# Kept experts: one output array for all scatters, each waiting for the last, in place of two arrays and a join

## The chip, the core and the metric

The kernel runs on one core of a Trainium2 chip. The metric is device time in microseconds (us); lower is better. TensorE (PE) multiplies, VectorE (DVE) and ScalarE (ACT) work element by element, GpSimd (POOL) does so too and builds the descriptors of indirect DMAs, SyncE (SP) issues plain DMAs.

## The reference, cut to what matters

The program is a network of four layers over 4096 tokens of 256 values: attention, a mixture of experts, a linear attention, and a second mixture of experts with 48 kept experts. Only the last one is touched in its arithmetic's order. With `T = 4096`, `CAP = 96`, `TOP_K = 8`:

```python
xb = zeros((E, CAP + 1, H)).at[flat_e, pos_c].set(x[tok])   # up to 96 tokens for each expert
g, u = split(einsum('ech,eoh->eco', xb, gate_up_proj), 2)
out = einsum('eci,ehi->ech', silu(g) * u, down_proj)
final = zeros_like(x).at[tok].add(y * w[:, None])           # a token may belong to 8 experts
x = x + final
```

So each expert's 96 rows are added to rows of one sum, and rows of different experts can be the same token.

## The kernel before

`front_phase` is the first part of the first mixture of experts. Its SP program loads weights, then clears rows of DRAM from the zeroed tile `front_zero`: the 96 spare rows of `out` and of `rows` (L889, L890), and the whole array `odd` (trace name `odd_sums`; L892 and L894, 4192 rows of 256 values). After them SP stores eight pieces of `roots` (L898), each once ACT has made it. At the phase's end SP waits for the clearing to have landed.

`ranking_phase` writes each token's row (256 values and its 48 weights) to `rows` (trace name `token_rows`), writes `x` to `out`, and makes `idx`, the list of 96 token numbers of each expert; places that are not used point to spare rows.

`kept_experts_phase` is the program's last phase. For each expert e of 48:

- POOL gathers 96 rows of `rows` into `xg` (L2860), six experts ahead of the scatter that stands before it in POOL's program;
- SP loads the expert's two weights, `kept_GU` of 192 KB and `kept_DN` of 96 KB, into one of 8 slots (L2844, L2845), once PE has used the slot's last ones (`pe_y`);
- PE transposes the rows (L2900), multiplies them by `GU` (L2910), then by `DN` (L2919); ACT copies and takes the silu; DVE makes `h` and then the weighted result `ys` (L2972);
- POOL scatters the 96 rows of `ys` with an add into DRAM (L2868): even experts into `out`, odd experts into `odd`.

POOL's program is written out in full: six gathers, then for each e: wait, scatter e, gather e+6 (none for the last six). The adds of one array must not overlap, since the same row may be in both; so scatter e waits for scatter e-2, the last one to the same array:

```python
if e >= 2:
    pool.wait_ge(added[e % 2], 16 * (e // 2))
scatter(e)
```

After the last scatter POOL waits for both arrays and issues four DMAs that add `odd` to `out` (L2887, 1 MB each), the join, and waits for them. The phase then ends with the semaphores' clearing and a barrier.

Of the kernel before, what the change touches and what calls it, by code (L numbers as in the profile page):

```python
# [16 lines left out]
F32 = mybir.dt.float32  # L17
# [4 lines left out]
ALU = mybir.AluOpType  # L22
# [4 lines left out]
D = 256  # L27
KD = D // P
BATCH, SEQ = 4, 1024
T = BATCH * SEQ  # L30
# [10 lines left out]
def done(step):  # L41

    return step + 1 + CREDIT
# [40 lines left out]
LH, LBLK = 16, 128  # L84
# [709 lines left out]
NW = LAT + SHARED  # L794


def front_phase(nc, a, AO, X, LH, LL, first_w, roots, ident, out, odd, rows):

    E, G, N = EXPERTS, GROUPS_E, PER_GROUP
    TAKEN = -3.0e38  # L800
# [3 lines left out]
    with Phase(nc, "front") as ph:  # L804
# [11 lines left out]
        zero = ph.sb("zero", [SPARE, ROW])  # L816
# [60 lines left out]
        @block.sync  # L877
        def _(sp):
            sp.dma_start(wo[:], a["L0_attn_W_O"].rearrange("(k p) n -> p k n", p=P)).then_inc(wo_in, 16)
            sp.dma_start(wu[:, :, 0:LAT], a["L0_ffn_fc1_w"].rearrange("(k p) n -> p k n", p=P)).then_inc(wu_in, 16)  # L880
            sp.dma_start(wu[:, :, LAT:NW], a["L0_ffn_shared_up_w"].rearrange("(k p) n -> p k n", p=P)).then_inc(wu_in, 16)
            sp.dma_start(wg[:], a["L0_ffn_gate_w"].rearrange("(k p) n -> p k n", p=P)).then_inc(wg_in, 16)
            sp.dma_start(down[:], a["L0_ffn_shared_down_w"].rearrange("(s p) n -> p s n", p=P)).then_inc(down_in, 16)
            sp.dma_start(bias_b[:, 0, :], a["L0_ffn_gate_bias"].rearrange("(o e) -> o e", o=1).to_broadcast([P, E]))\
                .then_inc(bias_in, 16)
            for to, source in first_w:
                sp.dma_start(to, source).then_inc(first_in, 16)
            sp.wait_ge(zeroed, 1)
            sp.dma_start(out[T:T + SPARE, :], zero[:, 0:D]).then_inc(cleared, 16)  # L889
            sp.dma_start(rows[T:T + SPARE, :], zero[:]).then_inc(cleared, 16)  # L890
            blank = zero[:, 0:D].rearrange("p (o n) -> p o n", o=1)
            sp.dma_start(odd[0:BLANKS * SPARE, :].rearrange("(t p) n -> p t n", p=SPARE),  # L892
                         blank.to_broadcast([SPARE, BLANKS, D])).then_inc(cleared, 16)
            sp.dma_start(odd[BLANKS * SPARE:T + SPARE, :], zero[0:T + SPARE - BLANKS * SPARE, 0:D])\  # L894
                .then_inc(cleared, 16)
            for c in range(CHUNKS):
                sp.wait_ge(act_ro, c + 1)
                sp.dma_start(roots[c], rootT[:, c % 2]).then_inc(stored[c % 2], 16)  # L898
            sp.wait_ge(first_in, 16 * len(first_w))
            sp.wait_ge(cleared, 64)  # L900
            sp.wait_ge(stored0, 8 * CHUNKS)
            sp.wait_ge(stored1, 8 * CHUNKS)

# [673 lines left out]
                out(2 * CHUNKS + half, half)  # L1577


def latent_moe_layer(nc, a, X, AO, held, ident, out, odd, rows):  # L1580

    with ExitStack() as c:
        LH = c.enter_context(nc.sbuf_tensor("B_LH", [P, T], F32R))
        LL = c.enter_context(nc.sbuf_tensor("B_LL", [P, T], F32R))
        wraw = c.enter_context(nc.sbuf_tensor("B_wraw", [P, 2, 2, WG, P], F32))
        fc2 = c.enter_context(nc.sbuf_tensor("B_fc2", [P, D], F32))
        roots = nc.dram_tensor("B_roots", (CHUNKS, EXPERTS, CHUNK), F32, kind="Internal").ap()
        views = (a["L0_ffn_w1"].rearrange("e l i -> l e i"), a["L0_ffn_w2"].rearrange("e i l -> i e l"))
        first = [(wraw[:, 0, w], views[w][:, 0:WG, :]) for w in range(2)]
        first += [(fc2[:], a["L0_ffn_fc2_w"])]  # L1590
        front_phase(nc, a, AO, X, LH, LL, first, roots, ident, out, odd, rows)
        held.close()
        W1H, W1L, W2H, W2L = (c.enter_context(nc.sbuf_tensor(f"B_{n}", [P, EXPERTS, P], F32R))
                              for n in ("W1H", "W1L", "W2H", "W2L"))
        experts_phase(nc, X, LH, LL, roots, views, wraw, fc2, W1H, W1L, W2H, W2L)
# [732 lines left out]
        linear_attention_phase(nc, X, XH, XL, ident, raw, wo_raw, dec_in, w_qkv, w_gate, w_out,  # L2328
                               a["L1_attn_rms_weight"], decays, kdec, bdec, acc, rs, x_rows, x_first, sums, later)
KEPT, OLD, WIDTH, CAP, TOP_D = 48, 128, 96, 96, 8  # L2330
BLANKS = (T + 96) // 96
ROW = D + KEPT
SLOTS = 8
JOINS = 4


def ranking_phase(nc, raw, o2n, x_first, acc, rs, sums, ident, rows, out, idx):
# [476 lines left out]
            tt(idx[:], tok[:], unused[:], ALU.add)  # L2814


def kept_experts_phase(nc, a, rows, out, odd, idx, ident):

    gu = a["L1_ffn_gate_up_proj"]
    dn = a["L1_ffn_down_proj"]  # L2820
# [1 line left out]
    with Phase(nc, "kept") as ph:  # L2822
# [9 lines left out]
        YP = ph.ps("YP", [CAP, 2, 512])  # L2832
        w_in = [ph.sem(f"w_in{u}") for u in range(S)]
        g_in = [ph.sem(f"g_in{u}") for u in range(S)]
        (pe_x, act_x, pe_gu, act_g, dve_h, pe_y, dve_y, added0, added1, joined, pool_turns) = ph.sems(
            "pe_x act_x pe_gu act_g dve_h pe_y dve_y added0 added1 joined pool_turns")
        added = (added0, added1)
        sums = (out, odd)
        block = ph.block()

        @block.sync
# [13 lines left out]
        @block.gpsimd  # L2855
        def _(pool):
            def gather(e):
                u = e % S

                nc.gpsimd.indirect_dma_start(out=xg[:, u], out_offset=None, in_=rows,  # L2860
                                             in_offset=bass.IndirectOffsetOnAxis(ap=idx[:, e:e + 1], axis=0))\
                    .then_inc(g_in[u], 16)

            def scatter(e):

                pool.wait_ge(dve_y, done(e))  # L2866

                nc.gpsimd.indirect_dma_start(out=sums[e % 2],  # L2868
                                             out_offset=bass.IndirectOffsetOnAxis(ap=idx[:, e:e + 1], axis=0),
                                             in_=ys[:, e % S], in_offset=None, compute_op=ALU.add)\  # L2870
                    .then_inc(added[e % 2], 16)

            for e in range(S - 2):
                gather(e)
            for e in range(KEPT):
                if e >= 2:
                    pool.wait_ge(added[e % 2], 16 * (e // 2))
                scatter(e)
                if e + S - 2 < KEPT:
                    gather(e + S - 2)  # L2880
            for u in range(S):
                pool.wait_ge(g_in[u], 16 * (KEPT // S))  # L2882
            for s in added:
                pool.wait_ge(s, 16 * (KEPT // 2))  # L2884
            parts = T // JOINS
            for j in range(JOINS):
                nc.gpsimd.dma_start(out[j * parts:(j + 1) * parts, :], odd[j * parts:(j + 1) * parts, :],  # L2887
                                    accum_op=ALU.add, max_dma_last_dim=8192).then_inc(joined, 16)
            pool.wait_ge(joined, 16 * JOINS)

        @block.tensor
        def _(pe):
# [80 lines left out]
                        .then_inc(dve_y, 1)  # L2973


def capacity_moe_layer(nc, a, x_first, ident, out, odd, rows, acc, rs, sums, raw, o2n):
    with ExitStack() as c:
        idx = c.enter_context(nc.sbuf_tensor("D_idx", [CAP, KEPT], U32))
        ranking_phase(nc, raw, o2n, x_first, acc, rs, sums, ident, rows, out, idx)
        kept_experts_phase(nc, a, rows, out, odd, idx, ident)  # L2980
def build_program(nc, a, out):
    x = a["L0_attn_x"].rearrange("b s d -> (b s) d")
    with ExitStack() as ctx:
        def keep(name, shape, dt=F32):
            return ctx.enter_context(nc.sbuf_tensor(name, shape, dt))

        X = keep("X", [P, TILES, D])
        x_at = nc.sbuf_base - TILES * D * 4
        ident = keep("ident", [P, P])
        kdec = keep("kdec", [P, LH])  # L2990
        bdec = keep("bdec", [P, LH])
        decays = nc.dram_tensor("decays", (LH, P, 2, LBLK), F32).ap()
        rows = nc.dram_tensor("token_rows", (T + SPARE, ROW), F32, kind="Internal").ap()
        odd = nc.dram_tensor("odd_sums", (T + SPARE, D), F32, kind="Internal").ap()
        held = ExitStack()
        AO = attention_layer(nc, a, x, X, held, ident, decays, kdec, bdec)
        latent_moe_layer(nc, a, X, AO, held, ident, out, odd, rows)
        raw = keep("D_w_gate", [P, KD, OLD])
        o2n = keep("D_o2n", [P, 1], I32)
        acc = nc.alloc_sbuf_tensor_at("C_acc", [P, TILES, D], F32, offset=x_at)  # L3000
        rs = keep("C_rs", [P, TILES])
        x_first = keep("D_x_first", [P, 2 * BATCH, D])
        sums = (keep("D_stats", [P, TILES, 6]), keep("D_mv", [P, TILES, 2]), keep("D_std", [P, TILES]),
                keep("D_rstd", [P, TILES]), keep("D_shift", [P, TILES]))
        x_rows = nc.dram_tensor("x_rows", (T, D), F32, kind="Internal").ap()
        linear_attention_layer(nc, a, X, ident, decays, kdec, bdec, acc, rs, raw, o2n, x_rows, x_first[:], sums)
        capacity_moe_layer(nc, a, x_first, ident, out, odd, rows, acc, rs, sums, raw, o2n)

# [3 lines left out]
SPARE = 96  # L3014
# [22 lines left out]
```

## Time and profile before

| | |
|---|---|
| median of 3 runs | 2849.91 us (2849.21 to 2852.32) |
| the profiled execution's own time | 2849.45 us |
| its span | 2847.1 us |
| PE busy | 2624.2 us (92%) |
| DVE busy | 1706.1 us (60%) |
| ACT busy | 1410.0 us (50%) |
| POOL busy | 786.6 us (28%) |
| last phase, from its first gather at 2666.94 us to the span's end | 180.2 us |

The busy shares are of the whole span; the change touches the last phase and some DMAs of the front phase, at about 606 us. There the stretches' own rows count, not the shares above.

### The profile page before, as it was taken

To read this page: it belongs to the slowest core of one execution; us is meant where nothing else is said; L and a number is where in the kernel's file an instruction comes from. 1 tells how busy PE (TensorE), PEld (TensorE's weight loads), DVE (VectorE), ACT (ScalarE), POOL (GpSimd) and SP (SyncE) were. 2 spreads that over 40 slices of the span, in tenths; PEclk is the share of its full clock that TensorE was granted. 3 is DMA by queue.
4 is the path that set the end of the run, shared out by engine and by line. 5 is a ranking of instruction groups with operands and counts; after the bars stand their busy time and mean duration, and the time that the engine had idled before them with its cause. 6 is when DMAs were issued, how large, how long until landed. Compare 5 with 4: busy or idle time off the path is not lost. (4 is left out here: it accounts for less than half of the span.)

```text
span 2847.1 us, 49896 instructions
## 1 busy us (share of the span) xinstructions
PE 2624.2 (92%) x17120; PEld 2103.3 (74%) x17120; DVE 1706.1 (60%) x3301; ACT 1410.0 (50%) x2606; POOL 786.6 (28%) x802
## 2 busy tenths in 40 slices
PE   7899999979979999899999999999999999986573
PEld 6444444448758888689998998989899899974452
DVE  7688888726678888665545545454544545567321
ACT  6477777766648878644333333333333333336310
POOL 3521212210052222122222222222222222224574
PEclk9799999989989999899999999999999999997665
DMA  8964645030055545422222222222222222223476
GB/s 253 214 109 63 84 70 81 14 102 3 4 194 179 192 184 189 139 49 50 74 50 59 53 60 49 49 61 51 58 50 66 46 50 61 47 74 124 115 169 125
DMA packets 409864, 260.98 MB, mean 92 GB/s; under 512 B 255904, under 2 KB 372032, under 8 KB 400896
## 3 DMA queue, kind: packets, MB, share of 16 engines
q1 hardware_dynamic: 401392, 243.59, 33.9%
q0 software_dynamic: 8256, 14.52, 3.0%
q8 instruction: 134, 2.20, 0.3%
q14 instruction: 82, 0.67, 0.1%
HBM read 182.09 MB, written 80.14 MB: 92 GB/s over the span
## 5 line engine op out<-in xcount | busy, mean ns | idle before, releaser
L1799 POOL TENSOR_TENSOR lin_o2sum<-lin_o2sum,lin_o 128x512 f32<-128x512 f32 x128 | 184.4, 1440 | 959.3 <-ACT lin_o L1863 959.3
L738 DVE TENSOR_REDUCE score_pm<-score_SM 128x1 f32<-128x512 f32 (+3 forms) x608 | 364.3, 655 | 80.6 <-PE score_SM L598 47.6
L692 ACT ACTIVATE score_PR<-score_SE 128x512 f32<-128x512 f32 (+1 forms) x640 | 309.7, 558 | 106.1 <-PE score_SE L626 102.4
L2136 DVE TENSOR_TENSOR C_acc<-lin_OUT,C_acc 128x512 f32<-128x512 f32 x240 | 165.2, 691 | 231.4 <-PE lin_OUT L1997 229.6
L1953 PE MATMUL lin_PJ<-C_XH,lin_WH 128*128 128x512 f32 x768 | 252.9, 410 | 2.1 <-DVE C_XL L2164 2.1
L1840 ACT ACTIVATE lin_qT<-lin_PJ 128x512 f32<-128x512 f32 x128 | 76.5, 598 | 353.5 <-PE lin_PJ L1953 353.5
L1953 PE MATMUL lin_PJ<-C_XL,lin_WH 128*128 128x512 f32 x768 | 240.7, 395 | 0.0
L598 PE MATMUL score_SM<-A_KR,A_QR 96*128 96x512 bf16 (+3 forms) x768 | 229.7, 340 | 11.7 <-DVEq L81 9.2
L1953 PE MATMUL lin_PJ<-C_XH,lin_WL 128*128 128x512 f32 x768 | 237.4, 390 | 0.0
L1868 ACT ACTIVATE lin_goh<-lin_go 128x512 fp32r<-128x512 f32 x128 | 81.0, 633 | 267.9 <-DVE lin_go L2272 267.9
L626 PE MATMUL score_SE<-A_QR,A_KR 99*128 99x512 bf16 (+3 forms) x768 | 210.4, 330 | 2.0 <-ACT score_PR L692 1.5
L2174 DVE STREAM_TRANSPOSE lin_kblk<-lin_kT 128x512 f32<-128x512 f32 x112 | 79.7, 711 | 214.8 <-ACT lin_kT L1844 214.5
L2063 PE MATMUL lin_O<-lin_sd,lin_v 128*128 128x128 f32 x1024 | 190.8, 276 | 9.8 <-POOL lin_qd L1794 4.2
L1499 ACT ACTIVATE experts_h<-experts_z 128x512 f32<-128x512 f32 x256 | 161.1, 629 | 70.7 <-DVE experts_z L1404 67.2
L1794 POOL TENSOR_TENSOR lin_qd<-lin_qT,lin_dec 128x512 f32<-128x512 f32 x128 | 165.0, 1289 | 72.0 <-DVE lin_dec L2236 72.0
L1404 DVE SCALAR_TENSOR_TENSOR experts_z<-experts_HP,experts_sq 128x512 f32<-128x512 f32 x256 | 173.9, 685 | 17.4 <-PE experts_HP L1536 14.3
L2063 PEld LDWEIGHTS lin_O<-lin_sd,lin_v 128*128 128x128 f32 x1024 | 158.2, 191 | 20.8 <-issue 13.7
L2066 PE MATMUL lin_O<-lin_qd,lin_kv 128*128 128x128 f32 x896 | 173.2, 275 | 0.0
L565 POOL TENSOR_SCALAR_AFFINE_SELECT score_PR<-score_PR 128x512 f32<-128x512 f32 x128 | 79.7, 635 | 333.5 <-ACT score_PR L692 333.5
L1953 PEld LDWEIGHTS lin_PJ<-C_XH,lin_WL 128*128 128x128 f32 x768 | 144.5, 188 | 34.1
L1953 PEld LDWEIGHTS lin_PJ<-C_XL,lin_WH 128*128 128x128 f32 x768 | 144.5, 188 | 34.0
L1411 DVE TENSOR_TENSOR experts_hl<-experts_h,experts_hh 128x512 fp32r<-128x512 f32 x192 | 139.1, 724 | 33.6 <-ACT experts_hh L1500 24.3
(372 smaller groups left out, 6488.7 us busy)
## 6 DMA issues: line engine op xcount, KB each, us to landing
experts_sq<-B_roots SPq DMA_DIRECT2D x64, 1024.0 KB, 4.7
k_turned<-lin_kblk SPq DMA_DIRECT2D x112, 256.0 KB, 2.0
lin_krow<-k_turned SPq DMA_DIRECT2D x448, 64.0 KB, 2.4
A_QR<-q_parts SPq DMA_DIRECT2D x96, 128.0 KB
A_KR<-k_parts SPq DMA_DIRECT2D x96, 128.0 KB
kept_GU<-L_ffn_gate_up_proj SPq DMA_DIRECT2D x48, 192.0 KB
v_rows<-inp_vt SPq DMA_DIRECT2D x32, 256.0 KB, 4.2
A_V<-v_rows SPq DMA_DIRECT2D x16, 512.0 KB
```

The costliest lines, as they stand in the source:

```text
L598: ins = nc.tensor.matmul(SM[:, count % RING, at:at + nk], QR[0:ROWS_QK, u, h0 + j, t * P:(t + 1) * P], KR[0:ROWS_QK, u, h0 + j, k0:k0 + nk ...
L626: ins = nc.tensor.matmul(SE[:, e % RING, at:at + nq], KR[0:ROWS_ALL, u, h, kt * P:(kt + 1) * P], QR[0:ROWS_ALL, u, h, q:q + nq], start=Tru ...
L692: nc.scalar.activation(PR[:, st % BUFS, h, 0:width], SE[:, e % RING, 0:width], ACT.Exp, scale=SCALE)\
L738: nc.vector.tensor_reduce(pm[:, n % 2, h0:h0 + nh, t, k0 // CHUNK], SM[:, count % RING, 0:nh * nk].rearrange("p (h k) -> p h k", h=nh), AX ...
L1404: nc.vector.scalar_tensor_tensor(z[:, e % 2], HP[:, e % BUFS], 0.0, sq[:, (e // QE) % BUFS, e % QE], ALU.max, ALU.mult).then_inc(dve_z, 1)
L1499: nc.scalar.activation(h[:, e % BUFS], z[:, e % 2], ACT.Square).then_inc(act_h, 1)
L1794: nc.gpsimd.tensor_tensor(qd[:], qT[:, j], dec[:, j, 0:1, :].to_broadcast([P, B4, BLK]), ALU.mult).then_inc(pool_qd, 1)
L1799: nc.gpsimd.tensor_tensor(o2sum[:, c], o2sum[:, c], o2[:], ALU.add).then_inc(pool_sum, 1)
L1953: ins = nc.tensor.matmul(PJ[:, bank], a[:, w, k, j * DH:(j + 1) * DH], x[:, k, :, c, :], start=(n == 0), stop=(n == 3 * KD - 1))
L2063: ins = nc.tensor.matmul(O[:, b, :], v[:, c % 2, b, j * DH:(j + 1) * DH], sd[:, b, :], start=True, stop=(c == 0))
L2066: ins = nc.tensor.matmul(O[:, b, :], kv[:, j, b, :], qd[:, b, :], start=False, stop=True)
L2136: nc.vector.tensor_tensor(dst, OUT[:, half], dst, ALU.add).then_inc(dve_acc[half], 1)
```

## The change

Every expert's scatter goes into `out`, and scatter e waits for scatter e-1. The array `odd` is gone, and with it the two DMAs that cleared it and the four that added it to `out`.

```diff
@@ front_phase, SP
             sp.dma_start(out[T:T + SPARE, :], zero[:, 0:D]).then_inc(cleared, 16)
             sp.dma_start(rows[T:T + SPARE, :], zero[:]).then_inc(cleared, 16)
-            blank = zero[:, 0:D].rearrange("p (o n) -> p o n", o=1)
-            sp.dma_start(odd[0:BLANKS * SPARE, :].rearrange("(t p) n -> p t n", p=SPARE),
-                         blank.to_broadcast([SPARE, BLANKS, D])).then_inc(cleared, 16)
-            sp.dma_start(odd[BLANKS * SPARE:T + SPARE, :], zero[0:T + SPARE - BLANKS * SPARE, 0:D])\
-                .then_inc(cleared, 16)
...
-            sp.wait_ge(cleared, 64)
+            sp.wait_ge(cleared, 32)
@@ kept_experts_phase, POOL
                 pool.wait_ge(dve_y, done(e))
 
-                nc.gpsimd.indirect_dma_start(out=sums[e % 2],
+                nc.gpsimd.indirect_dma_start(out=out,
                                              out_offset=bass.IndirectOffsetOnAxis(ap=idx[:, e:e + 1], axis=0),
                                              in_=ys[:, e % S], in_offset=None, compute_op=ALU.add)\
-                    .then_inc(added[e % 2], 16)
+                    .then_inc(added, 16)
...
             for e in range(KEPT):
-                if e >= 2:
-                    pool.wait_ge(added[e % 2], 16 * (e // 2))
+                if e:
+                    pool.wait_ge(added, 16 * e)
                 scatter(e)
                 if e + S - 2 < KEPT:
                     gather(e + S - 2)
             for u in range(S):
                 pool.wait_ge(g_in[u], 16 * (KEPT // S))
-            for s in added:
-                pool.wait_ge(s, 16 * (KEPT // 2))
-            parts = T // JOINS
-            for j in range(JOINS):
-                nc.gpsimd.dma_start(out[j * parts:(j + 1) * parts, :], odd[j * parts:(j + 1) * parts, :],
-                                    accum_op=ALU.add, max_dma_last_dim=8192).then_inc(joined, 16)
-            pool.wait_ge(joined, 16 * JOINS)
+            pool.wait_ge(added, 16 * KEPT)
```

This is how POOL's program ends before the change: the last two gathers, the last seven scatters with two destinations in turn, then the join.

```order
L2860 DMA kept_xg<-token_rows,D_idx 96x304
L2868 DMA odd_sums<-kept_ys,D_idx 4192x256
L2860 DMA kept_xg<-token_rows,D_idx 96x304
L2868 DMA out<-kept_ys,D_idx 4192x256
L2868 DMA odd_sums<-kept_ys,D_idx 4192x256
L2868 DMA out<-kept_ys,D_idx 4192x256
L2868 DMA odd_sums<-kept_ys,D_idx 4192x256
L2868 DMA out<-kept_ys,D_idx 4192x256
L2868 DMA odd_sums<-kept_ys,D_idx 4192x256
L2887 DMA out<-odd_sums 128x2048 x4
```

And this is the same place after it, in which the scatter's line is L2859 and the gather's L2851.

```order
L2851 DMA kept_xg<-token_rows,D_idx 96x304
L2859 DMA out<-kept_ys,D_idx 4192x256
L2851 DMA kept_xg<-token_rows,D_idx 96x304
L2859 DMA out<-kept_ys,D_idx 4192x256 x6
```

The order of gathers and scatters is the same; every scatter has one destination, so two in a row always share it, and nothing stands behind the last one.

## Rows read from the trace of the kernel before

**Rows 1.** Busy us (count) of PE, PEld, DVE, ACT, POOL; PEclk, DMA share, GB/s, one stretch:

```profile
2700.00:2740.00 40.00, 28.77 (x163) 20.95 (x163) 8.47 (x27) 6.28 (x27) 32.06 (x27) 0.71 0.80 175
```

**Rows 2.** POOL in order of time: start, duration, line, names, idle before and its releaser:

```profile
2678.99 1.52 POOL L2868 DMA_INDIRECT out<-kept_ys,D_idx  x1 [4.71 <-DVE kept_ys L2972]
...
2702.93 1.44 POOL L2868 DMA_INDIRECT out<-kept_ys,D_idx  x1 [0.30 <-issue]
...
2714.85 1.44 POOL L2868 DMA_INDIRECT out<-kept_ys,D_idx  x1 [0.30 <-issue]
...
2720.81 1.44 POOL L2868 DMA_INDIRECT out<-kept_ys,D_idx  x1 [0.31 <-DVE kept_ys L2972]
2722.55 0.93 POOL L2860 DMA_INDIRECT kept_xg<-token_rows,D_idx  x1 [0.30 <-issue]
2723.79 1.44 POOL L2868 DMA_INDIRECT odd_sums<-kept_ys,D_idx  x1 [0.31 <-DVE kept_ys L2972]
...
2804.25 1.44 POOL L2868 DMA_INDIRECT out<-kept_ys,D_idx  x1 [0.30 <-issue]
2805.99 1.43 POOL L2868 DMA_INDIRECT odd_sums<-kept_ys,D_idx  x1 [0.31 <-issue]
2807.90 1.40 POOL L2868 DMA_INDIRECT out<-kept_ys,D_idx  x1 [0.48 <-DMA out<-kept_ys,D_idx]
2809.81 1.40 POOL L2868 DMA_INDIRECT odd_sums<-kept_ys,D_idx  x1 [0.51 <-DMA odd_sums<-kept_ys,D_idx]
2812.06 1.40 POOL L2868 DMA_INDIRECT out<-kept_ys,D_idx  x1 [0.85 <-DVE kept_ys L2972]
2814.05 1.40 POOL L2868 DMA_INDIRECT odd_sums<-kept_ys,D_idx  x1 [0.58 <-issue]
```

**Rows 3.** The scatter's line, all 48: one of its waits (us, times), and issue to landing:

```profile
  DMA out<-kept_ys,D_idx: 0.5, 1
...
DMA to landing us min/median/max: 3.3/3.5/4.8
```

**Rows 4.** The chain that ended last, at the last scatter: start us, us, what:

```profile
2814.05 3.42 DMA odd_sums<-kept_ys,D_idx
...
2817.53 0.55 issue
```

**Rows 5.** The join's line: duration ns, first and last start; issue to landing:

```profile
L2887 POOL DMA_DIRECT2D out<-odd_sums x4: 919/1272/1492, 2818.1 to 2820.3; - x4
...
DMA to landing us min/median/max: 8.2/14.7/20.7
```

**Rows 6.** The page's first line:

```profile
span 2847.1 us, 49896 instructions
```

**Rows 7.** Landings of the scatters issued from 2702.9 to 2711.9 us (four):

```profile
DMA to landing us min/median/max: 4.1/4.3/4.6
```

**Rows 8.** The same for 2714.9 to 2729.7 us (six):

```profile
DMA to landing us min/median/max: 3.5/3.6/3.9
```

**Rows 9.** The same for 2804.2 to 2814.1 us (the last six):

```profile
DMA to landing us min/median/max: 3.3/3.4/3.4
```

**Rows 10.** SP's queue, the kept experts' weight loads in order of time:

```profile
2703.91 0.38 SPq L2844 DMA_DIRECT2D kept_GU<-L_ffn_gate_up_proj  x1
...
2717.30 0.38 SPq L2844 DMA_DIRECT2D kept_GU<-L_ffn_gate_up_proj  x1
```

**Rows 11.** SP's queue in the front phase:

```profile
606.47 13.91 SPq L894 DMA_DIRECT2D odd_sums<-front_zero  x1
697.86 102.40 SPq L898 DMA_DIRECT2D B_roots<-front_rootT  x8
```

**Rows 12.** Waits of 595 to 720 us: us in total, times, longest us:

```profile
PE front_TR L935 <- DVE front_AL L1166: 6.4, 1, 6.4
ACT front_WOH L1115 <- DMA front_wo<-L_attn_W_O: 5.2, 1, 5.2
```

More of the change, by code:

```diff
@@ L794, with front_phase @@
 NW = LAT + SHARED
-def front_phase(nc, a, AO, X, LH, LL, first_w, roots, ident, out, odd, rows):
+def front_phase(nc, a, AO, X, LH, LL, first_w, roots, ident, out, rows):
     E, G, N = EXPERTS, GROUPS_E, PER_GROUP
@@ L1577, in _, with latent_moe_layer @@
                 out(2 * CHUNKS + half, half)
-def latent_moe_layer(nc, a, X, AO, held, ident, out, odd, rows):
+def latent_moe_layer(nc, a, X, AO, held, ident, out, rows):
     with ExitStack() as c:
@@ L1590, in latent_moe_layer @@
         first += [(fc2[:], a["L0_ffn_fc2_w"])]
-        front_phase(nc, a, AO, X, LH, LL, first, roots, ident, out, odd, rows)
+        front_phase(nc, a, AO, X, LH, LL, first, roots, ident, out, rows)
         held.close()
@@ L2330 @@
 KEPT, OLD, WIDTH, CAP, TOP_D = 48, 128, 96, 96, 8
-BLANKS = (T + 96) // 96
 ROW = D + KEPT
 SLOTS = 8
-JOINS = 4
 def ranking_phase(nc, raw, o2n, x_first, acc, rs, sums, ident, rows, out, idx):
@@ L2814, in _, with kept_experts_phase @@
             tt(idx[:], tok[:], unused[:], ALU.add)
-def kept_experts_phase(nc, a, rows, out, odd, idx, ident):
+def kept_experts_phase(nc, a, rows, out, idx, ident):
     gu = a["L1_ffn_gate_up_proj"]
@@ L2834, in kept_experts_phase @@
         g_in = [ph.sem(f"g_in{u}") for u in range(S)]
[L2835 to L2838, printed above, removed]
+        (pe_x, act_x, pe_gu, act_g, dve_h, pe_y, dve_y, added) = ph.sems(
+            "pe_x act_x pe_gu act_g dve_h pe_y dve_y added")
         block = ph.block()
@@ L2973, in _, with capacity_moe_layer @@
                         .then_inc(dve_y, 1)
-def capacity_moe_layer(nc, a, x_first, ident, out, odd, rows, acc, rs, sums, raw, o2n):
+def capacity_moe_layer(nc, a, x_first, ident, out, rows, acc, rs, sums, raw, o2n):
     with ExitStack() as c:
@@ L2979, in capacity_moe_layer @@
         ranking_phase(nc, raw, o2n, x_first, acc, rs, sums, ident, rows, out, idx)
-        kept_experts_phase(nc, a, rows, out, odd, idx, ident)
+        kept_experts_phase(nc, a, rows, out, idx, ident)
 def build_program(nc, a, out):
@@ L2993, in build_program @@
         rows = nc.dram_tensor("token_rows", (T + SPARE, ROW), F32, kind="Internal").ap()
-        odd = nc.dram_tensor("odd_sums", (T + SPARE, D), F32, kind="Internal").ap()
         held = ExitStack()
         AO = attention_layer(nc, a, x, X, held, ident, decays, kdec, bdec)
-        latent_moe_layer(nc, a, X, AO, held, ident, out, odd, rows)
+        latent_moe_layer(nc, a, X, AO, held, ident, out, rows)
         raw = keep("D_w_gate", [P, KD, OLD])
@@ L3006, in build_program @@
         linear_attention_layer(nc, a, X, ident, decays, kdec, bdec, acc, rs, raw, o2n, x_rows, x_first[:], sums)
-        capacity_moe_layer(nc, a, x_first, ident, out, odd, rows, acc, rs, sums, raw, o2n)
+        capacity_moe_layer(nc, a, x_first, ident, out, rows, acc, rs, sums, raw, o2n)
 TRANSPOSED = ("L0_attn_W_Q", "L0_attn_W_K", "L0_attn_W_V", "L0_attn_W_O", "L0_ffn_gate_w", "L0_ffn_fc1_w",
```

## The prediction

> **What bounds the kernel now.** The change touches two places, so I read two stretches and not the shares of the whole span. First the chain of work that ended last: its end lies in the last phase, so what this phase gains or loses comes straight off the time. Then the busy table of a steady stretch of that phase [rows 1]. POOL is busy for 32.06 of 40 us, PE for 28.77, and neither alone looks full. POOL in order of time explains it [rows 2]: scatter 1.44 us, a gap of 0.30, gather 0.93, a gap of 0.31, next scatter. From 2720.81 to 2723.79 that is 2.98 us for an expert, and the gaps are put down to issuing or to a result that had come in the meantime. POOL issues back to back; it is the bound of this phase, and PE follows it. The first scatter starts at 2678.99, the last, 47 intervals later, at 2814.05: 135.06 us. Of these the last five, with no gather between, take 9.80 us (from 2804.25).
>
> The waits at the scatter's line come third: POOL waited there for an earlier scatter into the same array only at the very end, once in each array, the one shown being 0.5 us [rows 3]. With two arrays the wait is hidden: two intervals of 2.98 are 5.96 us, while a scatter lands 3.3 to 4.8 us after its issue, 3.5 in the median [rows 3]. That this is counted from the start of POOL's instruction and not from its end is seen in the chain: the last scatter starts at 2814.05 and its DMA takes 3.42 us, to 2817.47 [rows 4].
>
> **The change part by part.**
>
> *The new wait.* Scatter e may now start only when scatter e-1 has landed and POOL has noticed. Between the two stands one gather, whose 2.98 us no longer cover it. The new interval is landing L plus waking w. The trace has two such intervals in pure form, in the tail, where a scatter waited for the one of its own array: 2804.25 to 2807.90 is 3.65 us, and 2805.99 to 2809.81 is 3.82 [rows 2]. The landings there are 3.3 to 3.4 [rows 9], so w is about 0.25 and 0.42. Other wakings after a real pause: 0.55 us of issue behind the last landing [rows 4], and the scatter at 2812.06 with 0.85 us idle [rows 2]. I take w = 0.35, bounds 0.25 and 0.75.
>
> L is longer in the loop than in the tail. Read one by one, 13 of the 48 landings are 4.0 us or more; the other 35 average 3.5, all together 3.7. A group of each sort: 4.1 to 4.6 [rows 7] and 3.5 to 3.9 [rows 8]. What differs is when SP issues the next weights. In the first group that is about 1 us after the scatter (2702.93 and 2703.91), in the second about 2.4 us after (2714.85 and 2717.30) [rows 2, 10]; a load that falls into the scatter's own transfer stretches it by some 0.7 us. When SP issues depends on PE, which follows the gather issued right behind an earlier scatter; with another interval this offset changes, in a direction that I cannot fix. So I keep the mix of before, L = 3.7, and the interval is 3.7 + 0.35 = 4.05 us. Bounds: 3.65 from below, the shortest serial interval of the trace, and 3.7 + 0.75 = 4.45 from above.
>
> A rule speaks against this sum. The Trainium skill, page "DMA: Bandwidth & Descriptors", section "Anatomy of one DMA — SWDGE (gpsimd) path", gives a DMA issued from GpSimd about 2.0 us plus its bytes over 436 GB/s; 96 rows of 1 KB would by it take 2.2 us. If that ran from the issue, the gather would cover the wait and the loop would cost nothing. The trace has no landing below 3.3 us from the start of the instruction. Less POOL's 1.44 us there remain about 2 us, so the rule agrees with the trace only as the part behind POOL's own work. The row decides.
>
> The five last intervals have neither gathers nor loads beside them: the mean of the two pure ones, 3.74 us, each. Sum of the loop: 42 x 4.05 + 5 x 3.74 = 170.1 + 18.7 = 188.8 us, against 135.06: **+53.7 us**.
>
> What is queued behind the waiting scatter on POOL: gather e+6. It is issued right behind scatter e, so it comes later by the same delay; but it is six experts ahead, more than 24 us at the new pace, and what an expert needs from gather to `ys` is a landing of about 3.5 us and a few us of PE. Nobody waits that did not wait anyway. PE has 28.77 us of work in 40 now, and gets a third more time for each expert; even if its clock were granted lower more of the time than the 0.71 of now [rows 1], it stays behind POOL. Weight loads wait for PE, not the other way round. The eight slots of `ys` are not filled: DVE's result is then ready long before its scatter.
>
> *The join.* Its wait, its four DMAs and their landing go. The last of the four is issued at 2820.3, the longest landing is 20.7 us, that is 2841.0 [rows 5]; the span ends at 2847.1 [rows 6], so 6.1 us of closing stand behind it. From the last scatter's start to the span's end are now 33.05 us. After the change it is the landing of 3.4 and the same 6.1: 9.5 us. **-23.5 us**.
>
> *The clearing.* Two DMAs of SP in the front phase, of 4.1 MB together, go. The longer issue is 13.91 us on SP, but SP's next work is at 697.86 [rows 11], 77 us after it ended; this hides it. Who waited for a DMA there: ACT for `front_wo`, 5.2 us [rows 12], a load that stands ahead of the clearing in SP's queue and had landed before it began. PE's longest wait, 6.4 us, is for DVE, which followed ACT. I cost it at 0; without that cover it would be at most those 6.4 us, as a gain.
>
> *Sum.* 53.7 - 23.5 - 0 = +30.2 us on the profiled execution of 2849.45. The median of the runs is 2849.91, 0.46 above it, so the forecast is 2849.91 + 30.2 = **2880.1 us**, 1.1% slower. A measurement of this kernel tells 0.2% (5.7 us) from no change.
>
> **The rivals.**
>
> *The landings grow shorter (27 in 100).* A third more time for an expert thins the traffic (DMA share 0.80 now [rows 1]), and if the loads miss the scatter, L is 3.5 and the interval 3.85: 42 x 3.85 + 18.7 = 180.4, +45.3 - 23.5 = +21.8, 2871.7 us. At the lower bound, 47 x 3.65 = 171.6, it is +13.0, 2862.9.
>
> *The loads fall on every scatter (10 in 100).* PE's steps set when SP issues; if the offset locks at 1 us, L is 4.3 as in [rows 7] and the interval 4.65: 195.3 + 18.7 = 214.0, +78.9 - 23.5 = +55.4, 2905.3 us. Against it: in the trace of before the offset moved with PE's clock and no lock lasted. The same cost comes from waking always at its upper bound: 42 x 4.45 + 5 x 4.15 = 207.7, +49.1, 2899.0.
>
> *The wait is covered and the join's removal remains (3 in 100).* A landing below 2.98 - 0.25 = 2.7 us would leave the loop as it is: -23.5 us, 2826.4. This is the time by the rule above if it is counted from the issue. The mechanism decides from an interval of 2.87 + 23.5/47 = 3.37 us, 2.87 being the mean of the 47 now: below it the change is faster. The shortest serial interval of the trace is 3.65, in the tail where nothing else ran, and it would need a landing 0.3 us shorter than any of the 48.
>
> *The clearing did cost something (2 in 100).* Then up to 6.4 us come back at about 614 us: 2873.7. Against it stands the order of the waits above.
>
> **How the numbers follow.** My forecast has 58 in 100, with 27, 10, 3 and 2 for the others. The range runs from the shortest serial interval, 2863, to the upper bound of the waking, 2898; it takes in the first and the last rival, and leaves out half of the second, the third, and a little of the forecast's own margin at the ends. Faster by over 0.2%: 0.03. Within it, intervals of about 3.25 to 3.5 us: 0.01. Slower: 0.96.
>
> **What the changed kernel's profile would show.** POOL idle before nearly every scatter by about 1.4 us, released by the DMA of the scatter before (interval 4.05 less 2.98, and the usual 0.3); the last scatter near 2868 us; POOL's busy share down in the phase and PE's with it; no line for the join, and about 9.5 us from the last scatter to the end; the front phase the same, with SP's two issues gone. I am wrong in the size if the landings' median is far from 3.5 to 3.7, or the gap from landing to start far from 0.35; I am wrong in kind if POOL does not wait at the scatters, if the end behind the last one is much over 10 us, or if everything behind 620 us begins earlier.

## The result and the profile after

The changed kernel takes 2872.72 us (median of 4 runs, 2869.3 to 2873.57), the kernel before 2849.56 on the same chip: a ratio of 1.0075 [1.0063, 1.0088]. It is 23 us slower; 30 were forecast, in a range of 13 to 48.

The profiled execution took 2873.57 us, its span is 2871.9, 24.8 more than in [rows 6]. Where it went is read at three points of GpSimd's program: POOL in order of time, the changed kernel, with the same columns as [rows 2].

```profile
2680.72 1.52 POOL L2859 DMA_INDIRECT out<-kept_ys,D_idx  x1 [4.59 <-DVE kept_ys L2957]
...
2747.53 1.44 POOL L2859 DMA_INDIRECT out<-kept_ys,D_idx  x1 [1.19 <-DMA out<-kept_ys,D_idx]
2749.27 0.93 POOL L2851 DMA_INDIRECT kept_xg<-token_rows,D_idx  x1 [0.30 <-issue]
2751.24 1.44 POOL L2859 DMA_INDIRECT out<-kept_ys,D_idx  x1 [1.03 <-DMA out<-kept_ys,D_idx]
...
2841.44 1.44 POOL L2859 DMA_INDIRECT out<-kept_ys,D_idx  x1 [0.89 <-DMA out<-kept_ys,D_idx]
2844.99 1.43 POOL L2859 DMA_INDIRECT out<-kept_ys,D_idx  x1 [2.11 <-DMA out<-kept_ys,D_idx]
...
2859.52 1.40 POOL L2859 DMA_INDIRECT out<-kept_ys,D_idx  x1 [2.22 <-DMA out<-kept_ys,D_idx]
```

| stretch | before | after | difference |
|---|---|---|---|
| span's start to the first scatter | 2678.99 | 2680.72 | +1.7 |
| first scatter to last scatter | 135.06 | 178.80 | +43.7 |
| last scatter to the span's end | 33.05 | 12.38 | -20.7 |

The first row is no effect of the change: in the profiled executions of this study the first scatter starts anywhere between 2677.2 and 2684.0, in kernels whose program is the same up to there too. The other two make +23.1, where the medians differ by 23.2.

The gap before a scatter has changed its releaser. It was 0.30 us of issuing; from the tenth scatter on it is 0.9 to 1.4 where a gather stands between two scatters, and 2.1 to 2.2 in the last five, where none does, and it is ended by the DMA of the scatter before. The scatter's line, all 48, says the same in sum, with the landings below it:

```profile
  DMA out<-kept_ys,D_idx: 55.2, 43
...
DMA to landing us min/median/max: 3.3/3.4/4.8
```

Where [rows 3] had one wait of 0.5 us for the last DMA into `out`, there are 43 waits and 55.2 us. Four more gaps are put down to DVE, but they too end 0.2 to 0.3 us after the landing of the scatter before, and DVE had begun every result but the first at least 2.0 us ahead of its scatter. The chain that ended last runs through POOL alone in this stretch (start us, us, what):

```profile
2749.27 0.93 POOL kept_xg L2851
2750.20 0.80 issue
2751.00 0.02 POOLq L2857
2751.02 0.22 issue
2751.24 1.44 POOL out L2859
```

The semaphore's wait (L2857) ends at 2751.02, 3.49 us after the last scatter's start at 2747.53; 0.22 us later the next one starts. Landing and waking, 3.71 us, is the whole interval.

The steady stretch, with the columns of [rows 1]:

```profile
2700.00:2740.00 40.00, 29.02 (x128) 20.48 (x127) 6.93 (x21) 5.29 (x22) 24.52 (x22) 0.50 0.61 133
```

POOL's busy time falls from 32.06 to 24.52 us, the DMA share from 0.80 to 0.61. PE is busy for 29.02 as before, but with 128 matmuls in place of 163: the granted clock is 0.50 of 2.4 GHz, its lower level of 1.2 GHz, throughout, where it was 0.71 on average. Each matmul is slower. It costs the chain nothing here: 29.02 us for the 10.7 experts that 40 us hold at 3.74 us each are about 2.7 us of PE for an expert, an estimate from these two numbers, and that is less than an interval.

In the front phase SP's queue ends its first group of DMAs early, and its next work comes when it came before:

```profile
604.90 0.43 SPq L889 DMA_DIRECT2D out<-front_zero  x1
605.37 0.43 SPq L890 DMA_DIRECT2D token_rows<-front_zero  x1
698.13 0.32 SPq L893 DMA_DIRECT2D B_roots<-front_rootT  x1
```

From the phase's first DMA to the first stored `roots` are 101.6 us, and 101.5 before the change.

Last, the end. The queue instructions of the closing line in the last 12 us: ns, first and last start.

```profile
L57 POOLq COMPARE_BRANCH  x1: 41/41/41, 2862.9 to 2862.9; - x1
L57 POOLq DRAIN  x1: 7897/7897/7897, 2863.1 to 2863.1; - x1
```

POOL has nothing left at 2862.9, then drains for 7.90 us. In the kernel before the same instruction lasted 5.12:

```profile
L57 POOLq DRAIN  x1: 5120/5120/5120, 2841.2 to 2841.2; - x1
```

So the closing, from the last landing to the span's end, is 9.0 us in place of 6.1, and the join's removal gives 20.7 and not 23.5.

### The profile page after: what moved, and what is told of

It is laid out like the page before. It is cut to its first block and busy times, and to the rows that moved or that the text cites. A ratio compares the mean times of both kernels' runs of the same rounds, so it can differ in the third digit from the quotient of the medians.

```text
span 2871.9 us, 49890 instructions
## 1 busy us (share of the span) xinstructions
PE 2646.8 (92%) x17120; PEld 2118.8 (74%) x17120; DVE 1704.3 (59%) x3301; ACT 1410.1 (49%) x2606; POOL 783.2 (27%) x798
## 5 line engine op out<-in xcount | busy, mean ns | idle before, releaser
L1406 DVE TENSOR_TENSOR experts_hl<-experts_h,experts_hh 128x512 fp32r<-128x512 f32 x192 | 139.9, 729 | 33.3 <-ACT experts_hh L1495 24.8
```

## The experiments

Nine kernels ran. "Before" is the kernel before on the same chip in the same series. The changed kernel was not run again in these series, so comparisons with it rest on the loop, from the first scatter's start to the last one's, in the traces: in the five kernels whose scatters all wait for the last one and whose weight loads come as in the changed kernel it takes 177.7 to 178.9 us.

### Two arrays, serial wait

```diff
-                if e >= 2:
-                    pool.wait_ge(added[e % 2], 16 * (e // 2))
+                if e:
+                    pool.wait_ge(added[(e - 1) % 2], 16 * ((e + 1) // 2))
```

> Two arrays, their clearing and the join as before; only the wait is changed: each scatter waits for the last one, whichever array that went to. If the loop's loss is the wait alone (landing plus waking, about 3.8 us for an expert in place of 2.98), the interval from the first scatter to the last is that of the changed kernel, 179 us in place of 135, and the time is 2849.6 + 43.7 = 2893 us. If adds into one and the same array are what is slow (the RMW of rows that were just written), two arrays in turn stay near the time of before, 2850 us, or clearly under 2893.

2894.54 us against 2847.3: 1.0162 [1.0145, 1.0179]; the time is 1.5 us above the one expected, the difference 47 us, of which 2 are this series' faster kernel before. POOL in order of time:

```profile
2679.65 1.52 POOL L2868 DMA_INDIRECT out<-kept_ys,D_idx  x1 [4.24 <-DVE kept_ys L2972]
...
2746.40 1.44 POOL L2868 DMA_INDIRECT odd_sums<-kept_ys,D_idx  x1 [1.07 <-DMA out<-kept_ys,D_idx]
...
2858.53 1.40 POOL L2868 DMA_INDIRECT odd_sums<-kept_ys,D_idx  x1 [2.25 <-DMA out<-kept_ys,D_idx]
```

The loop takes 178.88 us, as in the changed kernel (178.80), though each scatter goes to the other array than the one it waits for. The wait alone makes the loss. Adds into one array in direct succession show no slowness of their own, within the 1.2 us by which such loops differ.

### Two arrays, no join

```diff
-            parts = T // JOINS
-            for j in range(JOINS):
-                nc.gpsimd.dma_start(out[j * parts:(j + 1) * parts, :], odd[j * parts:(j + 1) * parts, :],
-                                    accum_op=ALU.add, max_dma_last_dim=8192).then_inc(joined, 16)
-            pool.wait_ge(joined, 16 * JOINS)
```

> The kernel before without the four DMAs of the join; the sums of the odd experts are left out of the output. The changed kernel has 12.38 us from its last scatter's start to the end, the kernel before 33.05. If the end behind the last landing is a matter of what the program had done before, it is again about 9.1 us with a drain of about 7.9 us on GpSimd, and the time is 2849.6 - 20.7 = 2829 us. If the long drain belongs to the serial loop or to one array, it is 5.1 us as in the kernel before, and the time is 2826 us, the 23.5 us of the prediction.

2828.25 us against 2847.3: 0.9926 [0.9909, 0.9942], -19 us. From the last scatter (2815.98) to the span's end (2828.3) are 12.3 us, and the drain is the long one:

```profile
L57 POOLq DRAIN  x1: 7897/7897/7897, 2819.6 to 2819.6; - x1
```

The long drain belongs neither to the serial loop nor to the one array. Together with the run above the change is taken apart: +43.7 for the wait, -20.7 for the join, both read from traces. The medians of the two runs say it more coarsely, +47 and -19 us, each within about 5 us.

### One array, clearing put back

```diff
             sp.dma_start(rows[T:T + SPARE, :], zero[:]).then_inc(cleared, 16)
+            odd = nc.dram_tensor("odd_sums", (T + SPARE, D), F32, kind="Internal").ap()
...
+            sp.dma_start(odd[0:BLANKS * SPARE, :].rearrange("(t p) n -> p t n", p=SPARE),
+                         blank.to_broadcast([SPARE, BLANKS, D])).then_inc(cleared, 16)
+            sp.dma_start(odd[BLANKS * SPARE:T + SPARE, :], zero[0:T + SPARE - BLANKS * SPARE, 0:D])\
+                .then_inc(cleared, 16)
```

> The changed kernel with the two DMAs that clear the second array, which nothing uses, put back in the front phase. If the clearing was hidden, the time is that of the changed kernel, 2872.7 us, within 2 us, and the front phase lasts as long as in both traces (101.5 us from its first DMA to the first stored roots). If its 13.9 us of issuing and its 4.2 MB cost something, it is up to 6.4 us more.

2872.13 us, 1.0081 [1.0065, 1.0098] of before: the changed kernel's time. SP's queue:

```profile
607.39 14.47 SPq L896 DMA_DIRECT2D odd_sums<-front_zero  x1
698.21 0.33 SPq L900 DMA_DIRECT2D B_roots<-front_rootT  x1
```

SP is occupied with the issue for 14.47 us and has 76 us to spare. From the phase's first DMA to the first stored `roots` are 101.1 us, not more than without the clearing (101.6). The clearing cost nothing that this shows.

### One array, no later weight loads

```diff
-            with sp.Fori(0, KEPT // S - 1) as i:
-                for u in range(S):
-                    sp.wait_ge(pe_y, done(i * S + u))
-                    load((i + 1) * S + u, u)
...
-                pe.wait_ge(w_in[u], (i + 1) * 32)
+                pe.wait_ge(w_in[u], 32)
```

> The changed kernel, in which only the first eight experts' weights are loaded and all later experts use these; the other experts' weights are left out of the computation. If weight loads that fall into a scatter stretch its landing, the landings are 3.3 to 3.4 us throughout, the interval is 3.64 as in the tail, 47 of them are 171 us in place of 178.8, and the time is 2865 us. If the landings in the loop are long for another reason (the gathers' own traffic in the same queue), they stay at 3.5 us in the median of the loop and the time stays at 2872.

2867.23 us against 2847.3: 1.0067 [1.005, 1.0084]. The time is 2 us above the one expected. The first scatter starts at 2680.53, the last at 2851.95: 171.4 us, as expected. The stretch of 2700 to 2820, with the columns of [rows 1], and the landings of 22 scatters from 2721 to 2797.5:

```profile
2700.00:2820.00 120.00, 89.28 (x396) 63.80 (x394) 21.52 (x66) 15.90 (x66) 78.13 (x67) 0.50 0.37 59
```

```profile
DMA to landing us min/median/max: 3.3/3.4/3.4
```

The later loads' share in the changed loop is 7.4 us. Nearly half of it, 3.5 us, lies in the first nine intervals, in which the changed kernel has single landings of 4.1, 4.7 and 4.8 us. The amount of traffic also fell, from a DMA share of 0.61 to 0.37 in this stretch, so this run does not tell whether it is the amount or the moment.

### One array, later loads

```diff
                     sp.wait_ge(pe_y, done(i * S + u))
+                    sp.wait_ge(g_in[(u + 3) % S], (i + (u + 3) // S + 1) * 16)
                     load((i + 1) * S + u, u)
```

> The changed kernel, in which SP issues an expert's weight load about 1 us later: it waits also for the landing of one more gather. In the changed kernel a load is issued about 0.1 us before a scatter starts, and the landings of the loop are 3.5 us; loads issued 0.2 us or more after the scatter's start went with landings of 3.8 to 4.8 us. If the offset is the cause, it moves to between 0.1 and 0.9 us after the scatter's start, the landings to 3.8 to 4.2 us, the interval to 4.0 to 4.4, and 37 intervals cost 9 to 22 us: 2881 to 2894 us. If the landing depends on the amount of traffic and not on when it comes, the time stays at 2872.

2865.42 us against 2849.01: 1.0056 [1.0039, 1.0072]. It went the other way than I expected: faster than the changed kernel. The medians alone would leave some doubt, since the changed kernel's ratio is 1.0075 [1.0063, 1.0088] in its own series; but in the series of this run the kernel with a plain DMA last (below), whose loop is as in the changed kernel, took 2872.95 to 2875.7 us, and this one 2862.72 to 2869.36. SP's queue in the changed kernel:

```profile
2751.06 0.37 SPq L2835 DMA_DIRECT2D kept_GU<-L_ffn_gate_up_proj  x1
2754.82 0.37 SPq L2835 DMA_DIRECT2D kept_GU<-L_ffn_gate_up_proj  x1
```

Its scatters start at 2751.24 and 2754.99, so loads come 0.2 us ahead of them; the smaller load of each pair follows 0.56 us behind the larger one. In the run with the added wait, SP's queue, and below it POOL:

```profile
2751.02 0.37 SPq L2835 DMA_DIRECT2D kept_GU<-L_ffn_gate_up_proj  x1
2754.93 0.37 SPq L2835 DMA_DIRECT2D kept_GU<-L_ffn_gate_up_proj  x1
```

```profile
2748.95 1.44 POOL L2860 DMA_INDIRECT out<-kept_ys,D_idx  x1 [0.95 <-DMA out<-kept_ys,D_idx]
2752.58 1.44 POOL L2860 DMA_INDIRECT out<-kept_ys,D_idx  x1 [0.96 <-DMA out<-kept_ys,D_idx]
```

The load comes 2.1 and 2.4 us after these two scatters' starts, and 1.5 to 2.4 us after in the stretch read next, not 0.1 to 0.9 as I had put it. The landings of 22 scatters from 2719.6 to 2796.4, where 21 in the same stretch of the changed kernel have 3.4/3.5/3.7:

```profile
DMA to landing us min/median/max: 3.3/3.4/3.5
```

The loop is 2682.65 to 2854.31, 171.7 us, as if no weights were loaded at all, with all of them loaded: the DMA share from 2700 to 2820 is 0.63, where the changed kernel has 0.61. So it is the moment and not the amount. Of the 7.1 us, 3.4 lie in the first nine intervals, as in the run before. That SP's loads and GpSimd's scatters meet although different engines issue them is what the Trainium skill says on the page "DMA: Bandwidth & Descriptors", section "Issuing engines are not separate DMA queues"; both run on the same 16 DMA engines and interleave. The traces agree in so far as the moment of SP's loads alone moved GpSimd's loop by 7 us; which DMA engines the two shared was not read.

### Two arrays, later loads

The edit of the run above in the kernel before.

> The kernel before, two arrays and the join, with the later weight loads of the run before. There the later loads took the stretching out of the landings (3.6 to 3.4 us) and 7 us out of the serial loop. If a landing counts only where a scatter waits for the last one, the loop stays at 2.98 us for an expert, bound by GpSimd's issuing, whatever the landings are, and the time is that of the kernel before, 2848 us, within 2 us. If shorter landings or loads help otherwise, it is some us faster; if loads that come later hold PE up, slower.

2848.52 us against 2849.85: 0.9997 [0.9987, 1.0007]. The interval stays at 2.97 to 2.99 us in 41 of the 42 steps with a gather, while the landings, read one by one, still spread from 3.3 to 5.0 us. In this loop a landing does not count; it counts where a scatter waits for it.

### A plain DMA last

```diff
+            nc.gpsimd.dma_start(scratch[:], rows[T:T + SPARE, 0:D]).then_inc(tiny, 16)
             pool.wait_ge(added, 16 * KEPT)
+            pool.wait_ge(tiny, 16)
```

> The changed kernel with one small plain DMA of GpSimd (96 rows of 1 KB, DRAM to DRAM, into an array that nothing reads) issued behind the last scatter, landing beside it. GpSimd's drain at the phase's end lasts 7.90 us in the three kernels whose last DMA there was a scatter and 5.12 us in the two that end with the join. If a plain DMA behind the scatters shortens it, the drain is about 5.1 us and the time at most 2.8 us less than the changed kernel's, so 2870 us. If the drain counts the time since the scatters or the join's size, it stays at 7.9 and the time at 2873 to 2874.

2874.18 us against 2849.01: 1.0088 [1.0071, 1.0105]. The drain is not shorter:

```profile
L57 POOLq DRAIN  x1: 7978/7978/7978, 2864.2 to 2864.2; - x1
```

### Idle before the end

```diff
+            sp.wait_ge(added, 16 * KEPT)
+            sp.dma_start(scratch[:], rows[0:T, 0:D]).then_inc(copied, 16)
...
             pool.wait_ge(added, 16 * KEPT)
+            pool.wait_ge(copied, 16)
```

> The changed kernel, in which GpSimd, behind the last landing, waits for a plain copy of 4 MB from DRAM to DRAM that SP issues then, into an array that nothing reads. It is not meant to be fast (some 20 to 30 us more); the drain at the phase's end is read. If GpSimd's drain is shorter when it has stood idle for long since its last DMA, it lasts 5.12 us as behind the full join. If the join's own descriptors shorten it, it lasts 7.90 us as in the changed kernel.

One execution, 2893.48 us. The drain starts at 2882.7, 21 us after the last scatter's start at 2861.75, and lasts 7.90 us. So 21 us of idleness do not shorten it. What of the join does stays open.

### Two arrays, a join of 1024 rows

```diff
-            parts = T // JOINS
+            parts = 1024 // JOINS
```

> The kernel before, with a join over the first 1024 of the 4096 rows only: the sums of the odd experts in rows 1024 and up are left out of the output. The join's four landings came at steps of about 4.2 us for 1 MB each, 20.7 for the last. If the join's time goes with its bytes, a quarter leaves about 8 us from the last scatter's landing to the last of the join's, in place of 23.6, and the time is 2847.5 - 15.5 = 2832 us. If it is a fixed cost of four accumulating DMAs, the time is near the time of before, 2848 us. A join over only those rows which were touched would then beat both kernels.

2837.24 us against 2849.01: 0.9962 [0.9948, 0.9976], 12 us faster, not 16. The join's line:

```profile
L2887 POOL DMA_DIRECT2D out<-odd_sums x4: 887/1273/1702, 2817.2 to 2818.8; - x4
...
DMA to landing us min/median/max: 4.1/5.6/7.0
```

The last of its four starts at 2818.8 and lands 7.0 us later, where the full join needed 20.7 [rows 5]. The join's time goes mostly with its bytes: from these two sizes, an estimate of 4.6 us for each MB and 2.4 us besides. From the last scatter's landing to the join's last are 9.2 us, where 8 were expected and the full join has 23.5. A further part of the gain is given back by the drain, 8.22 us here. This is no version to use: on these inputs the experts' lists reach beyond row 1024, and in general any row can be in one.

## Why the prediction was right, step by step

**The bound.** Right. POOL's issuing bounds the loop of two arrays; with one array landing and waking do. The chain runs through POOL, and the serial wait alone gives the loss, with two arrays as well. But 58 in 100 stood on a landing of 3.7 us and an interval of 4.05, and neither came: the measured loop is that of the first rival, as shown below.

**The loop, +53.7.** The mechanism was right, the size 10.0 us too large: +43.7. The 42 intervals with a gather are 3.83 us in the mean (178.80 less 18.08 for the last five, over 42) and not 4.05. Of the 0.22 between them, 0.09 is waking: 0.26 us, between 0.22 and 0.31 in each of them with landings read to a tenth, against my 0.35. My value lay at the mean of the two intervals in the tail (0.25 and 0.42), and the second of these was not pure: POOL was still issuing another scatter until 2809.30, 0.51 us before this one started [rows 2], while in the changed loop POOL stands idle at each landing. The other two wakings that I listed are of another kind, one ahead of a plain DMA and one after DVE's result; they made only the upper bound. The other 0.14 is the landing: 3.56 in the mean of the 42 and not 3.7. The last five took 18.08 us against my 18.7.

**The landing's stretch.** I kept the mix of before because I could not fix where the loads would fall. The runs tell: PE follows the gathers, the gathers follow the scatters, so the load's offset settles, from about the tenth scatter on, between 0.4 us ahead of a scatter and about its start, with landings of 3.4 to 3.8. Within this band the offset already tells: loads issued 0.27 to 0.44 us ahead went with landings of 3.4 to 3.5, loads issued within 0.06 us of the start with 3.5 to 3.8. Before the change it came about 1 us after the scatter in one group and 2.4 after in another [rows 2, 10]. The rival in which it locks at 1 us did not come; the lock did, in a milder place. The stretch is worth 7 us in the changed kernel, nearly half of it before the offset has settled.

**What is queued behind.** Right: no result of DVE was late, each was begun 2 us and more ahead of its scatter but for the first, and PE, at a granted clock of 0.50, the lower of its two levels, from 2700 to 2820 us, still had slack.

**The join, -23.5.** 2.8 us too large: -20.7. I took the 6.1 us of closing as fixed. It holds GpSimd's drain, 5.12 us with the full join before it and 7.90 without, and these 2.78 us are the difference. The step that was off is the sentence that the same 6.1 stand behind the last scatter's landing.

**The clearing, 0.** Right, by the run that puts it back and by the front phase's length.

**The sum.** +30.2 less 10.0 plus 2.8 is +23.0, where +23 was measured. The two errors have opposite signs, so the total lies nearer to the forecast than its loop does; that part is luck. The loop's interval lay within its bounds of 3.65 and 4.45; to the closing I had given none, and it is the larger miss of the two in proportion: 9.0 us in place of 6.1, where the interval was 3.83 in place of 4.05.

**The rivals.** The shorter landings, 2871.7, came nearest in the time and nearest in the loop: its interval of 3.85 is 0.02 from the measured 3.83, mine 0.22. Its landing of 3.5 was a little short and its waking of 0.35 a little long (3.56 and 0.26 measured), and its time lacks the longer closing, so it too is partly right by cancelling. A covered wait did not come: the least of the 47 intervals is 3.55 us, above the 3.37 from which the change would pay. With the true closing that point is lower still, 2.87 + 20.7/47 = 3.31.

## What to carry to other kernels

A second destination that keeps two dependent DMAs in flight buys, at each step, the difference between landing plus waking and the issuing pace (44 us for 47 steps here), and costs a join that goes mostly with the array's bytes (21 us for 4 MB, with the shorter drain behind it counted). With these prices, and the loads moved out of the way, one array pays only below an estimated 23 steps: the last five, with no gather between, cost 8.4 of the 20.7 us (18.16 against 9.80), and the 12.3 left pay for 18 steps of 0.67 (3.65 against 2.98 us). Where a landing sets the pace, look at what other queues issue in its first microseconds: loads issued about 2 us later took 7 us out of the serial loop, and nothing out of the one in which the landing was hidden. What stands behind the removed work is not a constant: read what it consists of before adding it to a sum.

## What was not expected of the hardware

- GpSimd's drain at a phase's end is not constant: 5.12 us in all three kernels that end with a 4 MB join, 7.90 in the changed kernel and in five others that don't (among them one with two arrays and no join, and one after 21 us of idleness), 7.98 with a small plain DMA last, 8.22 with a join of 1 MB. Two guesses, the kind of the last DMA and idleness, were tested, each by one kernel, and fell; the cause is open.
- A stretch of a landing depends on the moment of other traffic to within some tenths: loads issued 0.2 us ahead of a scatter leave it at about 3.5 us, 1 us after it at 4.1 to 4.6 [rows 7, 10], 1.5 to 2.4 us after it, in the serial loop, at 3.3 to 3.5. In the loop of two arrays loads 2.1 to 2.5 us after a scatter went with 3.5 to 3.7 [rows 8]; there the next scatter follows within 1 us.
